# Attention and expert kernel: scores and row maximum one slot ahead, exponentials first on ScalarE, key transfers first in the queue, gathered rows weighted on ScalarE and summed in the transpose

## The reference, cut to what matters

```python
# x: (64, 128, 256); ctx: (64, 128, 192); 16 heads of 64; 8 experts of 256x256, top 2; all float32
q = layernorm(x) @ Wq                        # per batch element, 128 queries
k, v = split(ctx @ Wkv)                      # 128 keys and values
p = softmax(q k^T / 8)                       # per head, 128x128
x = x + (p v) @ Wproj + bproj
n = layernorm(x)
w, e = top2(softmax(n @ gate_w^T))           # two experts and weights for each of 8192 tokens
y = silu(n @ expert_w[e]^T + expert_b[e])    # for the two chosen
x = x + (w[0]*y[0] + w[1]*y[1]) @ combine_w^T
```

## Time and profile before

| | |
|---|---|
| median of three runs | 1970.71 us (1966.56 to 1971.49) |
| profiled execution | 1962.73 us, its span 1960.8 us |
| TensorE | 1601.6 us busy (82%) |
| VectorE | 1308.0 us (67%) |
| GpSimd | 1018.8 us (52%) |
| ScalarE | 998.9 us (51%) |
| mean granted TensorE clock | 0.926 |
| DMA | 303.77 MB, 155 GB/s |

### The profile page before, as it was taken

The page is one execution under the profiler, slowest core; times in us unless marked ns, Lnnn a source line. Parts: engine busy times, 40 slices in busy tenths (PEclk is TensorE's granted clock), DMA queues, the critical chain, the costliest instruction groups (busy, mean ns, idle before and its releaser), DMA issues.

```text
span 1960.8 us, 39159 instructions
## 1 busy us (share of the span) xinstructions
PE 1601.6 (82%) x11707; PEld 1505.6 (77%) x11707; DVE 1308.0 (67%) x3090; ACT 998.9 (51%) x2776; POOL 1018.8 (52%) x1277
## 2 busy tenths in 40 slices
PE   4688999988888888877889899887888897875663
PEld 4688888888888888777888788777788886874553
DVE  6478877786767777776677767867666677663221
ACT  4556666655546556544455555544455564541220
POOL 4445555554444445776444444777534457661164
PEclk9999999999999999988899999999999999995576
DMA  5633333334555653435465554355555544567783
GB/s 200 228 80 96 85 94 85 82 84 141 185 168 183 190 188 97 116 117 158 151 191 178 180 173 124 109 174 179 178 176 173 173 117 127 176 194 218 242 266 124
DMA packets 219977, 303.77 MB, mean 155 GB/s; under 512 B 24725, under 2 KB 184698, under 8 KB 219258
## 3 DMA queue, kind: packets, MB, share of 16 engines
q1 hardware_dynamic: 207482, 267.71, 45.2%
q0 software_dynamic: 12288, 33.57, 5.4%
HBM read 164.06 MB, written 70.01 MB: 119 GB/s over the span
## 4 chain that ended last, share of the span: by engine, by line
PE 34%; issue 16%; DVE 14%; POOL 11%; SPq 10%; DMA 9%; ACT 7%; ACTq 0%; DVEq 0%; POOLq 0%
PE gen_ps L482 9%; DMA k_s<-qk_s 7%; ACT probs L704 6%; PE s_ps L482 6%; PE proj_ps L482 5%; PE o_ps L482 5%; PE qk_ps L482 4%; DVE sums L859 4%; PE pT_ps L520 3%; POOL stage L1129 2%; POOL o_s_lo L1109 2%; DVE qk_s L810 2%; POOL probs L1098 2%; SPq L409 2%; SPq L358 2%
## 5 line engine op out<-in xcount | busy, mean ns | idle before, releaser
L1098 POOL TENSOR_TENSOR probs<-probs,inv_sums 128x512 f32<-128x512 f32 x256 | 267.0, 1043 | 547.1 <-DVE inv_sums L861 537.7
L852 DVE TENSOR_REDUCE neg_max<-s_ps 128x4 f32<-128x512 f32 x256 | 176.1, 688 | 240.2 <-PE s_ps L482 221.9
L677 ACT CAST pT_s_hi<-pT_ps 128x512 fp32r<-128x512 f32 x256 | 150.3, 587 | 362.9 <-PE pT_ps L520 344.8
L677 ACT COPY stage<-o_ps 64x256 f32<-64x256 f32 x512 | 188.1, 367 | 271.4 <-PE o_ps L482 252.8
L704 ACT ACTIVATE probs<-s_ps,neg_max 128x128 f32<-128x128 f32 x1024 | 293.0, 374 | 61.4 <-DVE neg_max L852 59.6
L482 PE MATMUL s_ps<-k_s,qk_s 128*128 128x256 f32 x1536 | 244.3, 298 | 66.5 <-DMA k_s<-qk_s 65.3
L482 PEld LDWEIGHTS s_ps<-k_s,qk_s 128*128 128x128 f32 x1536 | 214.4, 202 | 78.3 <-DMA k_s<-qk_s 78.0
L859 DVE TENSOR_REDUCE sums<-probs 128x4 f32<-128x512 f32 x256 | 175.8, 687 | 105.3 <-ACT probs L704 103.1
L482 PE MATMUL proj_ps<-wproj_s_hi,o_s_hi 128*128 128x256 f32 x512 | 159.9, 312 | 103.4 <-DVE x L889 53.0
L810 DVE TENSOR_TENSOR pT_s_lo<-pT_ps,pT_s_hi 128x512 fp32r<-128x512 f32 x256 | 176.5, 689 | 84.4 <-ACT pT_s_hi L677 72.8
L482 PEld LDWEIGHTS proj_ps<-wproj_s_hi,o_s_hi 128*128 128x128 f32 x512 | 99.5, 194 | 130.2 <-POOL o_s_lo L1109 65.0
(11 more groups left out here) (170 smaller groups left out, 4871.6 us busy)
## 6 DMA issues: line engine op xcount, KB each, us to landing
w_block<-expert_table SPq DMA_DIRECT2D x163, 512.0 KB
k_s<-qk_s SPq DMA_DIRECT2D x512, 128.0 KB
stage<-sorted_x SPq DMA_DIRECT2D x163, 128.0 KB
sorted_y<-stage SPq DMA_DIRECT2D x163, 128.0 KB
x_raw<-in_x SPq DMA_DIRECT2D x32, 256.0 KB
c_raw<-in_ctxT SPq DMA_DIRECT2D x32, 256.0 KB
stage<-in_x SPq DMA_DIRECT2D x32, 256.0 KB
x_kept<-x SPq DMA_DIRECT2D x32, 256.0 KB
```

Source lines behind the costliest of these rows:

```text
L677: last = act.copy(to, of)
L852: dve.tensor_reduce(neg_max[p % 2][:, :], s_ps[:, :].rearrange("p (k n) -> p k n", k=4), AX_X, ALU.max, negate=True).then_inc(max_done, 1)
L1098: pool.tensor_tensor(probs[b][:, :, :], probs[b][:, :, :], inv_sums[b][:, :].unsqueeze(2).broadcast_to([P, 4, P]), ALU.mult).then_inc(prob ...
```

## The change

- **Scores** of head pair u + 1 are made in slot u, after `project` and ahead of `attend`; its row maximum is taken in slot u on VectorE behind "mid".
- **ScalarE** does `exps(u)` ahead of `pT(u-1)`. VectorE begins a slot with `inverse(u)`, then `pT`, then `add_residual` (u = 2), and runs "mid" ahead of the row maximum and the norms.
- **SyncE** issues the key transfers first in its slot. They are still those for slot u + 1, which the scores now use in slot u.
- **Mixes**: ScalarE weights the gathered rows with four instructions of 128x256, behind "mid" and ahead of `attended`. The pairwise sum and its buffer are gone: eight transposing matmuls that accumulate in pairs take the place of four. 
- **Plan**: in attention there is one gather a slot, only in u = 4 to 7. By the new `room` the mixes lie 8 slots apart in 129, 137, ... 249 and 257, and then in 259, 261, 263, 265, 267 and 269; the last nine stay where they were, and so do all block slots and the last slot, 310.

```diff
@@ -66,7 +66,7 @@
...
                 if m >= 2:
-                    free = max(free, sorted(self.mix)[m - 2])
+                    free = max(free, sorted(self.mix)[m - 2] + 1)
                 for k in range(4):
@@ -97,7 +97,9 @@
...
         i, u = s // SLOTS, s % SLOTS
-        return 4 if i > pairs + 1 else 1 if u < 4 else 2
+        if i < pairs:
+            return 0 if u < 4 else 1
+        return 4 if i > pairs + 1 else 2
@@ -431,6 +432,10 @@
...
             for s, i, u in slots():
+                if exists(i) and u + 1 < SLOTS:
+                    spread_keys(i, u + 1)
+                if exists(i + 1) and u + 1 == SLOTS:
+                    spread_keys(i + 1, 0)
                 if u == 3 and exists(i):
@@ -439,10 +444,6 @@
...
                     sp.dma_start(x1_pairs[i - 1], x1[:, :, :]).then_inc(x1_saved, 16)
-                if exists(i) and u + 1 < SLOTS:
-                    spread_keys(i, u + 1)
-                if exists(i + 1) and u + 1 == SLOTS:
-                    spread_keys(i + 1, 0)
                 if u == 5 and i >= 0 and exists(i + 2):
@@ -562,6 +563,16 @@
...
+            def turn_sum(src, bank):
+
+                for t in range(2):
+                    for a in range(2):
+                        for k in range(2):
+                            mm = pe.matmul(bank[:, a * N2 + t * P:a * N2 + (t + 1) * P],
+                                           src[:, 2 * t + k, a * P:(a + 1) * P], ident[:, :], is_transpose=True,
+                                           start=k == 0, stop=k == 1)
+                return mm
+
             def turn(src, bank):
@@ -637,8 +648,8 @@
...
                     elif kind == "turn_mixed":
-                        pe.wait_ge(mixed_done, n + 1)
-                        mm = turn(mixed[n % 2], bank)
+                        pe.wait_ge(weighted, n + 1)
+                        mm = turn_sum(got[n % 2], bank)
                     else:
@@ -646,8 +657,6 @@
...
                 now, before, nxt = exists(i), exists(i - 1), exists(i + 1)
-                if now:
-                    scores(i, u)
                 if u == 0 and before:
@@ -662,6 +671,10 @@
...
                     project(i, u - 2)
+                if u < 7 and now:
+                    scores(i, u + 1)
+                if u == 7 and nxt:
+                    scores(i + 1, 0)
                 if u == 0 and before:
@@ -754,6 +767,13 @@
...
+            def weigh(m):
+                act.wait_ge(gathered[m % 2], 64 * (m // 2 + 1))
+                act.wait_ge(top_w_done, m + 1)
+                for k in range(4):
+                    last = act.activation(got[m % 2][:, k, :], got[m % 2][:, k, :], ACT.Copy, scale=top_w[:, m, k:k + 1])
+                last.then_inc(weighted, 1)
+
             def gate_exps(j):
@@ -767,12 +787,12 @@
...
                 now, before, nxt = exists(i), exists(i - 1), exists(i + 1)
+                if now:
+                    exps(i, u)
                 if u == 0 and before:
...
                     pT(i, u - 1)
-                if now:
-                    exps(i, u)
                 if s - 2 in plan.turn:
@@ -785,6 +805,8 @@
...
                 general(s, "mid")
+                if s in plan.mix:
+                    weigh(plan.mix[s])
                 if u == 0 and before:
@@ -1020,29 +1042,33 @@
...
                 if now:
-                    row_max(i, u)
+                    inverse(i, u)
                 if u == 0 and before:
...
                     pT(i, u - 1)
-                if now:
-                    inverse(i, u)
+                if u == 2 and before:
+                    add_residual(i - 1)
                 general(s, "early")
...
                     expert_out(plan.turn[s - 2][2])
+                if s - 3 in plan.mix:
+                    combined(plan.mix[s - 3])
                 if u < 6 and now:
...
                     qk(i + 1, u - 6)
-                if s - 3 in plan.mix:
-                    combined(plan.mix[s - 3])
+                general(s, "mid")
+                if u < 7 and now:
+                    row_max(i, u + 1)
+                if u == 7 and nxt:
+                    row_max(i + 1, 0)
                 if u == 0 and nxt:
...
                 if u == 2 and before:
-                    add_residual(i - 1)
                     dve.wait_ge(x1_done, i)
@@ -1059,7 +1085,6 @@
...
                     route_weights(i - 2)
-                general(s, "mid")
                 if i == -1 and u == 4:
@@ -1125,21 +1150,11 @@
...
                     pool.wait_ge(y_rows_done, c + 1)
-                    wait(pool, mixed_done, m - 1)
+                    wait(pool, made["turn_mixed"], m - 1)
                 pool.indirect_dma_start(
...
                         gathered[m % 2], 16)
-
-            def mix(m):
-                pool.wait_ge(gathered[m % 2], 64 * (m // 2 + 1))
-                pool.wait_ge(top_w_done, m + 1)
-                y = got[m % 2]
-                pool.tensor_tensor(y, y, top_w[:, m, :].unsqueeze(2).broadcast_to([P, 4, C]),
-                                   ALU.mult).then_inc(weighted, 1)
-                pool.wait_ge(weighted, m + 1)
-                wait(pool, made["turn_mixed"], m - 1)
-                pool.tensor_tensor(mixed[m % 2], y[:, 0:4:2, :], y[:, 1:4:2, :], ALU.add).then_inc(mixed_done, 1)
@@ -1171,8 +1186,6 @@
...
                     rsqrt(i - 1, 1)
-                if s in plan.mix:
-                    mix(plan.mix[s])
                 if u < 4 and exists(i - 2):
```

More of the change, by code:

```diff
@@ L197, in xattn_moe_kernel @@
         x1_back = [carve(2 * C, 1) for _ in range(2)]
-        mixed = [carve(C, 2) for _ in range(2)]
         x_block = [carve(C, 1) for _ in range(RING)]
@@ L201, in xattn_moe_kernel @@
         th = [carve(C, 1) for _ in range(2)]
-        assert taken[0] == 6 * D
+        taken[0] = 6 * D
         o_full = carve(P, 2)
@@ L295, in xattn_moe_kernel @@
         ctx_rest = sem("ctx_rest")
-        ctx_lo, probs_done, weighted, mixed_done = (
-            sem(n) for n in ("ctx_lo", "probs_done", "weighted", "mixed_done"))
+        ctx_lo, probs_done, weighted = (
+            sem(n) for n in ("ctx_lo", "probs_done", "weighted"))
         eps_done = [sem(f"eps_done{n}") for n in (1, 2)]
```

## The result

The changed kernel takes 2207.68 us (median of 4 runs, 2202.6 to 2208.5) against 1971.1 us (1966.56 to 1972.45) for the kernel before: ratio 1.1207, interval 1.1175 to 1.1239. It is 12.1% slower; the forecast was 3.3% slower (2036 us), and the top of its range was 2115 us. The profiled execution has a span of 2204.3 us, 243.5 more than before.

The account below looks back on a forecast made before the run. TensorE nearly bounds attention without blocks; no engine is full throughout. Terms 100 + 40 - 83 - 8 + 11 + 6 = +66 us on 1962.73 gave 2029, 8 more for the median: 2036 us, range 1955 to 2115.

Parts of the forecast that it names:

- The loop the prediction draws: Block slots: expert's end, 1.7 us to key issue, 4.0 transfer, 2.54 scores to next expert's end; nothing overlaps.
- The signs it named for the ring: Changed trace: block slots 8 us or more, nearly alike; key wait some 200 us; clock about 0.9 or less.
- the ring: That loop through the key transfer in 112 block slots: 8.2 us each at least, +100 us (bounds +60 to +170).
- 112 x 8.2: Sizing of the block slots: 112 slots at 8.2 us make 918 against 818.8 us, +100 us.
- +40: Clock term: TensorE idles, then half clock costs 1 us in three block slots of eight; bounds 0 and +110.
- the half clock feeds the ring: Rival: most block slots pay 1 us and more, 9.2 us a slot, +212 - 80, 2100 us; chance 0.19.
- Mixes: 63 slots between block stretches: GpSimd stalls go, 357 instead of 440.2 us, -83 us (bounds -95 and -60).
- Other slots: 130 slots: residual wait may go, keys wanted 1.4 us earlier; -8 us, between -57 and +25.
- The rival in which VectorE becomes the bound: Slots without blocks: ScalarE or VectorE becomes the bound, 0.5 us a slot in 130 slots, 2100 us; chance 0.08.
- Start: Slots 0 to 7: scores and `attend` join SyncE's chain of weight stores and key transfers, +11 us (0 to +20).
- Tail: Six more mixes in slots 257 to 269, +13, less GpSimd's part, -7: +6 us (bounds -10 and +25).
- the ring is short enough: Rival: block slots below 7.97 us without half clocks make the change faster; at 7.6 some 1928 us; chance 0.17.

Follow-up runs that it names:

- e1: Changed kernel, but SyncE issues the keys of slot s + 2 in slot s, ahead of its wait for the expert matmuls: 1868.03 us, ratio 0.9474.
- e4: Changed kernel, but VectorE takes the second norm's statistics ahead of "mid" and the row maximum again: 2166.8 us, ratio 1.0977.
- e5: Changed kernel plus 2 to 18 unread filler matmuls on TensorE ahead of its wait for keys, in block slots only: 2149.76 us, ratio 1.0971.
- e7: Changed kernel with only the first of the two 128 KB key transfers per head pair, the second head's keys left out: 2085.96 us, ratio 1.0632.
- e2: Kernel before plus the mix part of the change alone, scores and key order as before: 1903.16 us, ratio 0.9662.
- e3: Kernel before plus the order part of the change alone, mixes still on GpSimd in their old slots: 2241.48 us, ratio 1.1384.
- e6: Changed kernel with the edits of e1 and e4 together: 1796.98 us, ratio 0.9160.
- e8: Kernel before, old order of scores, plus the mix part, the early residual and SyncE's list of e1: 1795.97 us, ratio 0.9165.

## Why the prediction was wrong, point by point

**Direction and mechanism: right.** The loop the prediction draws is there row for row (1.70 + 4.33 + 2.54), SyncE's part is nearly what it was before, and e1 removes the loop and all it cost. The signs it named for the ring came: slots over 8 us, a grown wait for keys (269.3 us on the matmuls and 297.5 on the weight loads, for some 200), 1.7 us and some 4 us, and a clock of 0.89 to 0.92. Others did not. `project` was to wait no longer for GpSimd, and its wait on `o_s_lo` went from 49.6 to 71.1 us, for the reason that e4 shows. The wait on `add_residual` was to go and kept 17.2 us. And block slots were to be nearly alike whatever their u: the ring's mean is 9.1 to 9.5 us for six of the eight, but 10.6 in u = 3 and 8.5 in u = 4.

The span grew by 243.5 us for the forecast's 66. Of the 178 us between them some 87 are the ring's, 38 the mixes', 26 those of the other slots, 16 the start's and 11 the tail's.

**The step that failed** is the sizing of the ring, "112 x 8.2" and "+40", which measured +227.5 instead of +140. Against 8.2 + 0.36 the 111 slots show:

- Issue 1.81 instead of 1.7: 0.11 x 111 = 12 us.
- Transfer 4.40 instead of 4.0: 44 us. The prediction took 3.80, one of the rows in which TensorE waited, plus 0.2. But the change also altered the transfer's neighbours. In u = 3 the residual's load and store, 256 KB each, are now issued right behind the keys, and there the mean is 5.11 us; in u = 5 it is 4.59, in u = 2 4.49, elsewhere 4.16 to 4.24, so that these three hold about half of the 44 us, and the rest is the 0.2 us by which all others exceed 4.0. SyncE of the kernel after in slot 91, u = 3, and then TensorE's scores:

```profile
632.80 1.26 SPq L359 DMA_DIRECT2D k_s<-qk_s  x2
634.12 0.62 SPq L443 DMA_DIRECT2D stage<-in_x  x1
634.78 0.83 SPq L446 DMA_DIRECT2D x_kept<-x  x1
635.66 0.54 SPq L421 DMA_DIRECT2D sorted_y<-stage  x1
```

```profile
638.76 1.65 PE L483 MATMUL s_ps<-k_s,qk_s 128*128 128x256 f32 x6 [2.81 <-DMA k_s<-qk_s]
```

Those scores start 5.96 us behind the issue. "Key transfers first in the queue" means that others are right behind them, and the rows are consistent with sharing of the DMA engines; no run moved the neighbours alone, and in e4, where SyncE's list is the same, the mean of u = 3 is 4.62 instead of 5.11. So how much of the 0.4 us is theirs stays open.
- Half clock 0.64 instead of 0.36 us a slot: 31 us, and 71 in all. The prediction had three slots of eight and got 56 of 111. The rival that fed on this ("the half clock feeds the ring", 2100 us) named the right thing and was near in the ring (+212 us, 9.2 us a slot), but kept the forecast's other terms, which were too low (its -80 should have been their sum, -74); e5 shows its cause and, less the longer transfer, its price.

These make 87 us, to rounding the whole difference between 140 and 227.5.

The Trainium skill ("DMA: Bandwidth & Descriptors", section "Anatomy of one DMA — SWDGE (gpsimd) path") would have had 2.9 us for the two issues, an estimate by its fit for DMAs that GpSimd issues; SyncE issues these, and no slot was below 3.73. By the page's figures the fixed part, about 2.0 us, outweighs the bytes here (some 0.3 us for 128 KB, an estimate), and e7 agrees in kind: half the bytes still took 3.83 us.

**Mixes: right in kind, -45 instead of -83.** e2 gives 61 us for these stretches without the order part. Of the remaining 16 us, 13 are the norm's wait: with e4's edit the stretches are at -58; the last 3 have no owner. The other 22 us were never there: with the mix part alone these 64 slots take 446.2 - 61 = 385 us, for the forecast's 357 and the 6 of slot 116. Half of it is the price of a plain slot, 5.30 us from one favourable stretch of 32 where slots 13 to 79 averaged 367.3 / 67 = 5.48 (0.18 x 64, some 12 us); the rest has no measured owner.

**Other slots: the sign was wrong, +18 in slots 13 to 79 alone instead of -8 for all.** The prediction followed `add_residual` and the keys, and was right on both (53.0 to 17.2 us; no ring over two slots). It did not follow what stands *behind* the moved `row_max` and "mid": the second norm's statistics, for which GpSimd waits with a scatter and the split behind it. The diff shows these lines as untouched context, and that is how they were missed. e4 shows it: the 18 us are down to 1.9, and the whole kernel gains some 45. The rival in which VectorE becomes the bound is not this: VectorE is busy 275.9 of 385.3 us there; its order costs, not its load.

**Start: +27 instead of +11.** SyncE's stores of expert weights stand in the ring in the first pair as the expert's loads do later, and e1, which puts the keys ahead of them too, brings the start back to 82.0 us against 84.1 before. The prediction had the chain, but charged it only with the scores and `attend`; what the other 16 us are was not followed row by row.

**Tail: +17 instead of +6.** It belongs to the mix part: e2 alone has +14.6, and e3, without it, 0.0. Which of that part's edits costs it is not shown.

**Rival "the ring is short enough":** its threshold was 7.97 us a slot, and the ring's shortest transfer alone would have given about 1.8 + 3.73 + 2.54 = 8.1. Even the shortest transfer in every slot would not have reached it.

## What to carry to other kernels

When an edit moves a consumer one step ahead, write down what its producer's queue has to finish first. If that includes a wait for the consumer's engine, the step has become a loop, its length is the sum of its latencies, and busy shares show nothing of it (TensorE is at 77%); issuing the keys ahead of that wait removed 340 us here. In a list that several engines share, price the lines that now stand behind the moved one, even where the diff shows them unchanged. And once the transfers came early enough, scores ahead or not made no difference in sum (e6 and e8, 0.916 both): the gain to be had, 8.4% below the kernel before, was in SyncE's order, the early residual and the mixes.

## What the runs showed of the hardware

- Work that does nothing made the program faster. With fillers of 0.4 to 2.3 us a slot, the first block stretch went from a granted clock of 0.91 and 328.6 us to 1.00 and 310.4.
- Idle stretches of nearly one length are not alike: behind one of 2.72 us the granted clock was 0.57, behind one of 2.81 us it was 1.00. 56 of 111 slots had the long work, and TensorE had stood still longer ahead of their scores (2.91 us on average, 1.79 in the others); what decides in the single slot stays open.
- Between buffers of the core's own memory, 128 KB took 3.83 us on average from issue to use (e7), and twice as much in two issues 4.40 us in the kernel after.
